# GpSimd's gathers wait for set-up jobs and moment steps: a DLRM tower with a CIN layer on one core

## What is computed

```python
e = jnp.stack([tbl_0[ids[:, 0]], ..., tbl_25[ids[:, 25]]], axis=1)      # 512 x 26 x 32
x1 = einsum('bik,bjk,hij->bhk', e,  e, W1) + b1[None, :, None]          # 128 x 26 x 26 weights
x2 = einsum('bik,bjk,hij->bhk', x1, e, W2) + b2[None, :, None]          # 128 x 128 x 26 weights
z  = sum(concatenate([x1, x2], axis=1), axis=-1)                        # 512 x 256
h  = relu(concatenate([z, dense_ctx], axis=1) @ W_top1 + b_top1)        # 272 -> 512
h  = relu(h @ W_top2 + b_top2)                                          # 512 -> 256
y  = h @ W_top3
```

## Time and profile before

| | us |
|---|---|
| median of 3 runs | 290.71 (289.09 to 292.08) |
| profiled execution, device time | 289.82 |
| its span, first to last instruction | 288.1 |

### The profile page before, as it was taken

The page is one execution under the profiler, slowest core; times in us unless marked ns, Lnnn a source line. Parts: engine busy times, 40 slices in busy tenths (PEclk is TensorE's granted clock), DMA queues, the critical chain, the costliest instruction groups (busy, mean ns, idle before and its releaser), DMA issues.

```text
span 288.1 us, 3079 instructions
## 1 busy us (share of the span) xinstructions
PE 161.0 (56%) x1193; PEld 146.8 (51%) x1193; DVE 97.5 (34%) x341; ACT 56.7 (20%) x156; POOL 100.1 (35%) x110
## 2 busy tenths in 40 slices
PE   8764221121111111111114449799999999999996
PEld 8753221011010101011014339799999999999995
DVE  2400000000000302100019996499249826973100
ACT  1021000000000000000032423602450245026312
POOL 5777777777777777774000000000000000000000
PEclk9995555555555555555555769979999999999999
DMA  6910110001101101100000000000000000000000
GB/s 228 354 17 12 14 15 14 12 14 14 14 12 14 14 11 15 14 13 9 0 0 0 0 0 3 1 2 0 2 0 2 0 2 1 2 0 2 2 0 0
DMA packets 5217, 5.97 MB, mean 21 GB/s; under 512 B 2226, under 2 KB 4402, under 8 KB 5203
## 3 DMA queue, kind: packets, MB, share of 16 engines
q0 software_dynamic: 3328, 1.71, 4.2%
q1 hardware_dynamic: 1410, 2.52, 2.7%
q10 hardware_dynamic: 464, 1.54, 1.5%
HBM read 5.77 MB, written 0.00 MB: 20 GB/s over the span
## 4 chain that ended last, share of the span: by engine, by line
PE 42%; another core or an unknown queue 35%; DVE 8%; issue 8%; ACT 3%; DMA 3%; SPq 0%
PE bank L252 12%; PE bank L253 6%; PE bank L259 5%; PE bank L263 4%; DVE folded L497 4%; PE bank L219 3%; DMA w2t<-in_w2t_dram 3%; PE bank L266 3%; PE bank L298 3%; PE bank L285 2%; PE bank L283 2%; ACT folded L345 1%; DVE diag L459 1%; PE bank L288 1%
## 5 line engine op out<-in xcount | busy, mean ns | idle before, releaser
L199 POOL DMA_INDIRECT rows<-in_tbl_dram,idx x104 | 99.4, 956 | 32.9 <-issue 31.4
L224 PE MATMUL bank<-w1s,w2t 128*128 128x169 f32 x52 | 21.9, 473 | 100.4 <-issue 97.1
L224 PEld LDWEIGHTS bank<-w1s,w2t 128*128 128x128 f32 x52 | 14.5, 301 | 107.4 <-issue 103.6
L252 PE MATMUL bank<-diag,prod 128*128 128x108 f32 x256 | 49.3, 293 | 1.4 <-DVE prod L623 1.4
L497 DVE TENSOR_TENSOR folded<-folded 128x6 f32<-128x6 f32 (+15 forms) x44 | 5.6, 177 | 108.6 <-issue 99.5
L252 PEld LDWEIGHTS bank<-diag,prod 128*128 128x128 f32 x256 | 38.8, 192 | 1.8 <-ACT v L351 1.8
L253 PE MATMUL bank<-diag,prod 128*77 128x64 f32 x256 | 36.9, 226 | 0.0
L253 PEld LDWEIGHTS bank<-diag,prod 128*77 128x77 f32 x256 | 30.9, 148 | 0.0
L486 DVE COPY t<-bank 13x128 f32<-13x128 f32 (+1 forms) x64 | 16.8, 263 | 31.7 <-PE bank L253 31.0
L345 ACT COPY folded<-bank 128x366 f32<-128x366 f32 x13 | 6.0, 465 | 84.1 <-remote 65.4
L373 ACT COPY t<-bank 55x256 f32<-55x256 f32 (+2 forms) x48 | 14.1, 294 | 28.2 <-PE bank L253 27.9
(11 more groups left out here) (55 smaller groups left out, 168.3 us busy)
## 6 DMA issues: line engine op xcount, KB each, us to landing
rows<-in_tbl_dram,idx POOLq DMA_INDIRECT x104
wt<-in_W_top_dram SPq DMA_DIRECT2D x2, 512.0 KB
w2t<-in_w2t_dram ACTq DMA_DIRECT2D x1, 832.0 KB
w2t<-in_w2t_dram SPq DMA_DIRECT2D x1, 832.0 KB
w1t<-in_w1t_dram ACTq DMA_DIRECT2D x1, 640.0 KB
w1p<-in_w1p_dram SPq DMA_DIRECT2D x1, 521.0 KB
idx<-in_ids_dram SPq DMA_DIRECT2D x1, 39.0 KB
dctx<-in_dctx_dram ACTq DMA_DIRECT2D x1, 32.0 KB
```

Of the source, the lines that this page charges most:

```text
L199: pool.indirect_dma_start(rows[t][:, f, :], None, tables[f], bass.IndirectOffsetOnAxis(ap=idx[:, t, f:f + 1], axis=0)).then_inc(s_got[t][p ...
L224: mm = nc.tensor.matmul(ps[:, i * CROSS:(i + 1) * CROSS], w2t[:, lo + x0 + i, :], w1s[:, c0:c0 + CROSS], start=True, stop=True)
L252: nc.tensor.matmul(m0[:, a0:a0 + JW * QUADS], prod[:, G, 0:P], mov, start=True, stop=True)
```

## The change

Two tables say what a gather waits for. Before gather (tile t, field f), GpSimd waits until `s_sf`, the number of set-up jobs that ACT has copied, has reached AFTER_SETUP[t, f]. For tile 1 AFTER_STEP[0] and for tiles 2 and 3 AFTER_STEP[1] give the moment steps of tile t - 1 that have to be done before field f. All gathers are issued in the same order as before, into the same buffers; nothing else is touched.

```diff
+AFTER_SETUP = {(0, 13): 6, (0, 18): 13, (0, 22): 18, (1, 0): 23, (1, 6): 27, (1, 12): 31}
+AFTER_STEP = [{18: 1, 22: 2, 25: 3}, {8: 1, 12: 2, 16: 3, 20: 4}]
...
                 for part, (f0, f1, _) in enumerate(PARTS):
                     for f in range(f0, f1):
+                        if (t, f) in AFTER_SETUP:
+                            pool.wait_ge(s_sf, AFTER_SETUP[t, f])
+                        if t and f in AFTER_STEP[t > 1]:
+                            pool.wait_ge(s_mom, (t - 1) * STEPS + AFTER_STEP[t > 1][f])
                         pool.indirect_dma_start(
                             rows[t][:, f, :], None, tables[f],
                             bass.IndirectOffsetOnAxis(ap=idx[:, t, f:f + 1], axis=0)).then_inc(s_got[t][part], 16)
```

## The result

| | us |
|---|---|
| before, median of 4 runs | 289.9 (288.33 to 292.08) |
| after, median of 4 runs | 232.5 (229.19 to 238.43) |
| ratio | 0.795, interval 0.782 to 0.808 |
| profiled execution of after, and its span | 229.19, 227.5 |

The ratio compares the faster executions alone, since in some of them a kernel of this kind takes a per cent or more longer. The change makes the kernel 20% faster, on the chip of this comparison. Both belong to the result.

What follows compares the result with a forecast made beforehand. It took a report path shared with the gathers, about 1.4 us each, to bound the first half and PE the last part. Set-up 69 + moments 115.2 + 42 lost + 1.7 outside the span gave 228 us, range 180 to 265.

Steps and rivals of the forecast that it cites:

- The reading of the slow stretch: Up to 149 us: gathers put about 1.4 us each on a shared report path, and others' share falls with stream length.
- Set-up: From the start to tile 0's first moment matmul: 69 us forecast against 172.85, bounds 53 and about 85.
- The first wait: GpSimd's wait in the set-up for six copied jobs, after 13 gathers: over at 22.6 us.
- One sign named in the prediction: ACT's copies of set-up jobs should come under 2.9 us apart.
- Moments: After the first moment matmul: 60 gathers losing 0.70 us each add 42 us to 115.2, ends 0 and 73.
- 110 ns an instruction: Report pace of PE's instructions early in a stream, used to price a gather in the moments at 0.70 us.
- The tile lengths: In the moments, tiles 0 to 2 should last 38 to 46 us and tile 3 near 30.
- Rival 1: Short bursts harmless, moments start near 53 us, then GpSimd bounds and tile 3 is late: 179 us; chance 0.26.
- Rival 2: Bursts join and the others' share falls as before, 1.21 us for each of 60 gathers: 258 to 275 us; chance 0.16.
- Rival 3: Slow pace is the set-up's own, not the gathers': 298 us; chance 0.08 together with Rival 4's upper end.
- Rival 4: Each gather costs everyone 1.21 us anywhere: 282 us, or 14 more; chance 0.04 near no change, upper end within 0.08.
- theory B: Set up for the experiments, not the prediction: each gather costs PE a fixed 0.74 us wherever it stands.

Runs made afterwards that it cites:

- The run at 1.55 us apart: Kernel before with a memset and a wait for the one in front behind each gather, no other waits: 215.8 us against 287.9, ratio 0.751.
- second comparison: The changed kernel run again on another chip, against the kernel before at 185.6 us there: 185.5 us, ratio 0.999.

## Why the prediction was right, and where it was not

228 us were forecast and 232.5 measured; the profiled execution took 229.19.

**The reading of the slow stretch** held. The 1.40 us a gather from the end at 148.97 came out again for 44, 66 and 104 gathers, and the falling share with the length of a stream is what the set-up waits alone and the step waits alone showed. That a gather needs 1.40 us of the path holds on some chips only, which no row of before could tell.

**Set-up**: 69 us forecast, 62.7 measured. The first wait came out exactly (22.6 forecast for the gather of field 13, 22.80 measured). The step that failed is the pace after it: I let jobs pass at 1.42 us in the pause and in the next burst, where the backlog was gone within 2 us and nine copies came at once (21.70). The waits for 13 and 18 jobs were therefore over before they counted, and four pauses became two. DVE's 23 us chain was hardly slowed: it reached its last products at 62.05. I had eighteen gathers costing it 7 us after 56; instead the gathers beside it were the ones that took longer (2.06 to 3.79 us). One sign named in the prediction failed: the copies stay under 2.9 us apart up to 29.93, but those beside the second burst come 5.0 and 6.4 us apart (29.93, 34.93, 41.33).

**Moments**: 42 us lost over 60 gathers forecast, 49.6 over 67 measured; 0.70 against 0.74 us a gather. By tile it is 0.81, 0.64 and 0.79 us. The sum is near, but its form is not a law: reports cost hardly anything at 1.50 and 1.55 us apart, and 84 us over 64 gathers in the run with the set-up waits only. Nor was the price well founded. The 110 ns an instruction was read from the 11.45 us up to the first copy, which hold 1.88 us in which PE waited for w2t before its first fold matmul at 11.79. The run at 1.55 us apart, where the fold copies come 0.62 us apart from the first on, has its first gather at 2.89 and its first copy at 12.97: the same sum gives 97 ns there, and a loss of 0.63 us a gather where none was lost. So the agreement of 0.70 with 0.74 is luck; that bursts of 4 to 16 gathers cost about this much is what the runs showed, not what the row could tell. A part of it is the clock, which I had left out: in tiles 0 to 2 the granted clock was 0.78 to 0.81 against 0.98 in the earlier trace rows. Where PE had been held up it went on for a while near the lower of its two levels, 1.2 of 2.4 GHz (granted clock 0.53 from 153.7 to 157.4); the chain of after has two groups there,

```profile
155.06 0.51 PE bank L261 x2
155.80 0.51 PE bank L261 x2
```

0.74 us for a group against 0.385. How much of the 49.6 us it makes was not worked out.

**The errors** of 6 us in the set-up (too high) and of 8 us in the moments (too low) go against each other, so the forecast of the whole is closer than its parts, which is luck as well.

**The tile lengths**: 38 to 46 us forecast, 46.9 (just above), 43.9 and 41.4 measured, tile 3 32.6 for "near 30". PE lost its time inside the bursts and hardly any in the pauses, as named. The gathers came in time.

**Rival 1** (179 us, GpSimd the bound) did not come true on this chip, but it is close to what the kernel does on the chip of its second comparison: 185.5 us with the first moment at 50.2. **Rival 2** is what happens with the step waits left out (265.7). **Rival 3** (the slow pace is the set-up's own) does not hold where before takes 285 to 290 us: there the copies came together when GpSimd fell silent, in the midst of the set-up (21.70), and moment steps are held up as well (61 us). The Trainium skill, page "SBUF — State Buffer", section "Who interferes with whom", says of SBUF's ports that PE and ACT never wait; carried over to the reports of their instructions it fails there, while on the chips where before takes 185 us the runs agree with it. **Rival 4** falls with theory B.

**Open.** What the path is. It goes by gathers and not by rows. At either size a gather makes the same 32 packets (3328 on the software queue in both pages) and adds 16 to its semaphore, so either would fit; late in a long stream PE gets one instruction through per 1.40 us. The Trainium skill, page "NOTIFIC — the notification-queue block", section "Interfaces", says that the block which writes the engines' trace and event records can hold up the engines that send them when an inner FIFO is full; no run here shows whether this is that, and since every execution here has its span and clock on record, none shows whether the slowing is there when nothing is recorded. Why chips differ was not found either. No chip is known to have been used in more than one set of runs, so a lasting property of the chip can't be told from its condition at that time. A kernel with tile 0's gathers only was not run.

## What to carry to other kernels

When engines with nothing to wait for go at one odd, fixed pace, divide the length of the slow stretch by the number of requests that another engine issued in it. If that gives the same time (here 1.40 us both ways), look at the distance between the requests before cutting them into bursts. A steady distance just above what the path takes (1.50 us here, 0.739 of before's time) did better than waits that stop and release bursts at full rate (0.795), but both pay only on a chip that has the limit, so measure the kernel before beside every run and compare on more than one chip. A price per request that was read from one length of stream says nothing about another.

## What the runs showed of the hardware

- In four of six sets of runs, on one core each, the kernel before took 285 to 290 us; in the other two, on two other chips, the same kernel took 185 us, and kernels with the same gathers had their reports at PE's pace there, but for the first few copies of some (up to 1.2 us apart in place of 0.6).
- On the slower chips a gather takes 1.40 us of something that PE and DVE need to report the end of an instruction: slow stretches behind 44, 66 and 104 gathers all end at that count, and 64 rows in place of 128 change nothing. That it is the report which is late is inferred from copies that start long after PE's matmuls.
- PE can issue far ahead of its reports: ten fold jobs were issued by 18.57 us in before, while the eighth was told at 37.63.
- A backlog is worked off soon after GpSimd stops, in a time that grows with the stream: about 2 us after 13 gathers, 6 us after 44, 15 us after 104.
- The distance decides: at 1.28 us apart fold copies came 9 us apart, at 1.40 us moment steps 9 to 14, at 1.50 us some 4.1 and 4.3, and at 1.55 us, but for one, 3.0 to 3.1, which is PE's own pace.
